# Attention loop on one Trainium2 core: products with the values moved in front of the scores

## What is computed

```python
def proj(W, b):
    return (x @ W.T + b).reshape(Bb, Ss, H, DH).transpose(0, 2, 1, 3)
Q, K, V = (proj(Wq, bq), proj(Wk, bk), proj(Wv, bv))
...
scores = jnp.einsum('bhqd,bhkd->bhqk', Q, K) * scale
...
bias = lam[:, None, None, None] * prior_bias[None, None]
dense_out = jnp.einsum('bhqk,bhkd->bhqd', jax.nn.softmax(scores + bias, axis=-1), V)
...
out = out.transpose(0, 2, 1, 3).reshape(Bb, Ss, Dd)
return out @ Wo.T + bo
```

## Time and profile before

| | |
|---|---|
| median of three runs | 1857.48 us (1856.89 to 1862.09) |
| the profiled execution | 1869.88 us, its span 1868.1 us |
| TensorE | busy 1800.2 us, 96% of the span, mean granted clock 0.979 |
| VectorE | busy 1077.9 us, 58% |
| ScalarE | busy 926.0 us, 50% |
| GpSimd | busy 561.3 us, 30% |
| attention loop | 725.3 to about 1247 us of the span, 256 steps |
| in the window 725 to 1250 us | TensorE busy 514.54 us, VectorE 443.28, ScalarE 446.85 |

### The profile page before, as it was taken

One profiled execution on the slowest core, in us unless ns is written; L12 is line 12 of the kernel. 1 busy time (PEld: TensorE's weight loads), 2 busy tenths in 40 slices (PEclk: granted clock), 3 DMA queues, 4 the chain that ended last, 5 costly groups with the idle time before them and its releaser, 6 DMA issues.

```text
span 1868.1 us, 41317 instructions
## 1 busy us (share of the span) xinstructions
PE 1800.2 (96%) x17131; PEld 1288.8 (69%) x17131; DVE 1077.9 (58%) x2319; ACT 926.0 (50%) x1697; POOL 561.3 (30%) x966
## 2 busy tenths in 40 slices
PE   7989999999999988999999999999999999999997
PEld 3657768565657645777777777766777777777775
DVE  5674644172241256888888788853555544445453
ACT  2313231213343235888888888854555544445512
POOL 3262130042130352121212121103555443455413
PEclk8989999999999989999999999999999999999998
DMA  6100002113353569611113010000000000010001
GB/s 189 26 24 1 4 2 69 72 54 116 102 179 92 162 184 170 95 35 30 33 29 111 21 41 22 22 24 1 2 2 2 2 2 2 2 30 2 2 0 45
DMA packets 89948, 93.55 MB, mean 50 GB/s; under 512 B 35282, under 2 KB 75154, under 8 KB 89618
## 3 DMA queue, kind: packets, MB, share of 16 engines
q1 hardware_dynamic: 83506, 79.12, 15.7%
q0 software_dynamic: 3456, 9.44, 1.9%
q10 hardware_dynamic: 2800, 2.34, 0.4%
HBM read 68.34 MB, written 23.07 MB: 49 GB/s over the span
## 4 chain that ended last, share of the span: by engine, by line
PE 89%; DVE 5%; ACT 2%; DMA 2%; issue 1%; POOL 1%; SPq 0%; POOLq 0%; DVEq 0%; ACTq 0%
PE PS L1870 13%; PE PS L1250 8%; PE PS L1884 7%; PE PS L1259 7%; PE PS L2209 6%; PE PS L1861 6%; PE PS L2287 5%; PE PS L2264 4%; PE PS L2214 3%; PE PS L2248 3%; PE PS L615 2%; PE PS L707 2%; PE PS L2294 2%; PE PS L2326 2%; PE PS L714 2%; PE PS L562 1%
## 5 line engine op out<-in xcount | busy, mean ns | idle before, releaser
L2043 DVE CUSTOM_DVE_ANT_0 arena<-PS,arena 128x1024 f32<-128x1024 f32 x256 | 312.0, 1219 | 63.9 <-PE PS L1861 60.0
L1964 ACT ACTIVATE arena<-arena 128x1024 f32<-128x1024 f32 x256 | 296.7, 1159 | 9.4 <-DVE arena L2043 9.2
L1870 PE MATMUL PS<-arena 128*128 128x128 f32 x2048 | 279.8, 279 | 2.3 <-issue 1.9
L1870 PEld LDWEIGHTS PS<-arena 128*128 128x128 f32 x2048 | 230.5, 142 | 60.2 <-issue 27.0
L2491 POOL TENSOR_SCALAR arena<-arena 128x384 f32<-128x384 f32 (+1 forms) x256 | 143.4, 573 | 251.4 <-DVE arena L2400 251.4
L2372 ACT ACTIVATE arena<-arena 128x385 f32<-128x385 f32 (+1 forms) x256 | 151.4, 593 | 128.6 <-DVE arena L2409 128.6
L1960 ACT COPY arena<-PS 128x512 f32<-128x512 f32 x298 | 170.0, 585 | 63.3 <-PE PS L1870 60.9
L1861 PE MATMUL PS<-arena 96*128 96x512 bf16 x512 | 154.9, 384 | 4.9 <-DVE arena L2043 3.8
L2409 DVE CUSTOM_DVE_ANT_0 arena<-PS,arena 128x384 f32<-128x384 f32 (+1 forms) x256 | 123.2, 538 | 52.3 <-PE PS L2251 39.9
L1250 PE MATMUL PS<-arena 128*128 128x512 f32 x320 | 143.6, 606 | 6.6 <-ACT arena L1395 5.9
L2050 DVE COPY arena<-PS 128x512 f32<-128x512 f32 x214 | 146.9, 687 | 2.3 <-PE PS L1870 2.1
(11 more groups left out here) (340 smaller groups left out, 3079.4 us busy)
## 6 DMA issues: line engine op xcount, KB each, us to landing
arena<-in_L_ffn_W SPq DMA_DIRECT2D x16, 1024.0 KB, 7.5
arena<-prior SPq DMA_DIRECT2D x16, 512.0 KB, 4.2
parts<-arena SPq DMA_DIRECT2D x24, 256.0 KB, 5.1
arena<-parts SPq DMA_DIRECT2D x96, 64.0 KB, 2.9
arena<-parts SPq DMA_DIRECT2D x48, 128.0 KB, 10.6
prior<-arena SPq DMA_DIRECT2D x4, 1024.0 KB, 6.7
ye<-arena SPq DMA_DIRECT2D x7, 512.0 KB, 3.0
ya<-arena SPq DMA_DIRECT2D x7, 512.0 KB, 5.0
```

Source lines behind the costliest of these rows:

```text
L1870: h = e.transpose(PS[:, i, P * j:P * j + P], Sb[z % 3][:, 512 * g + P * j:512 * g + P * j + P], ident)
L1964: e.activation(Sb[z % 3], Sb[z % 3], ACT.Exp, bias=mr[:, z % 4:z % 4 + 1], scale=-1.0).then_inc(s_exp, 1)
L2043: e.tensor_tensor_reduce(Sb[z % 3], ps, Ab[m % 2], 1.0, 3e38, ALU.add, ALU.min, mr[:, z % 4:z % 4 + 1]).then_inc(s_ttr, 1)
```

## The change

In a step with products with the values, TensorE runs them ahead of the scores of that step, and the scores then stand directly ahead of the turn. Before, they stood between the scores and the turn. The instructions are the same, and so is the order on every other engine. In steps without such products (the even ones, and those up to 6), nothing moves.

```diff
         for z in range(NZ + 15):
+            if summed(z):
+                values(*summed(z))
             if z < NZ:
                 scores(z)
-            if summed(z):
-                values(*summed(z))
             if 2 <= z < NZ + 2:
                 turn(z - 2)
             if gathered(z) is not None:
```

## The result

| | before | changed |
|---|---|---|
| median, 20 runs each | 1862.28 us (1856.89 to 1866.73) | 1866.09 us (1862.99 to 1871.78) |
| ratio | 1 | 1.0025, 95% interval 1.0017 to 1.0034 |
| profiled execution's span | 1868.1 us | 1864.1 us |
| V of z = 7 to V of z = 255, in the trace | 492.78 us | 495.32 us |

A forecast was written before the change was run, and what follows sets the result against it. TensorE, busy throughout the attention loop, was taken as the bound. The terms -3.1 + 6.0 + 1.3 + 2.1 gave +6.3 us on the three-run median of 1857.48, so 1863.8, likeliest 1864, range 1855 to 1872.

The forecast's parts named there:

- The case forecast: Attention loop: small crossing gain outweighed by waits, +6.3 us or +0.34%; chance 0.55.
- three places: Waits at the banks of turns' first halves (+6.0 us), two double steps (+1.3), small copy of sums (+2.1).
- the ten steps: Steps z = 23, 39, 71, 87, 119, 143, 147, 183, 215, 231: TensorE idle about 0.6 us each for VectorE's copy.
- crossing, 125 pairs: From products with the values into scores: bare weight load 0.03 instead of 0.06, pair 3.80 to 3.77, -3.1 us.
- bank behind the late copy, 10 pairs: Gather and small closing steps: the even step's turn waits 0.60 us for VectorE's late copy, 6.0 us in all.
- z = 135 and z = 167: Two double steps: closing pieces wait longer on VectorE, +0.5 us at z = 135, +0.75 at z = 167, together +1.3.
- small copy ahead, 14 pairs: ScalarE's small copy of the sums delays its two turn copies by 0.15 us in 14 steps, 2.1 us.
- a load wholly hidden: Faster bound of the crossing term: no weight load lies bare ahead of the scores, -7.1 us.
- its row for the 0.03: First score of the loop: its matmul follows its load by 0.03 us, taken as the bare load.
- The rival of the waiting V: Next products with the values wait for VectorE's copy in 42 pairs, 0.1 us each, 4 us more: 1868; chance 0.15.
- Nothing moves: Same work, two shape crossings per pair, bank waits taken up: time stays at 1857.5 us; chance 0.20.
- The way out is cheap: Values to scores costs no pause or load: 0.15 us saved per pair, 18.8 less 9.4 of waits, 1848; chance 0.10.

The follow-up runs named there:

- e6_only_bank: Changed kernel, ScalarE copying first halves of turns only in gather and closing steps, VectorE in all others; ratio to the kernel before 0.9972, measured again 0.9957.
- e8_before_only: Kernel before with copies dealt out as in e6_only_bank, differing from it only in the place of the scores; ratio to before 0.9996, again 0.9984.
- e1_bank_copies: Changed kernel, ScalarE also copying the turn's first half where a gather or small closing piece takes a bank behind it; ratio to the kernel before 0.9986.
- e7_vector_first: Changed kernel, VectorE copying the turn ahead of the bias step in gather and small closing steps; ratio to the kernel before 1.0009.
- e4_before_both: Kernel before with the edits of e1_bank_copies and e2_sums_later; ratio to the unedited kernel before 1.0007.
- e2_sums_later: Changed kernel, ScalarE's small copy of the sums issued behind the copies of the turn; ratio to the kernel before 1.0009.
- e5_split: e6_only_bank with the products with the values cut in two halves, one ahead of the scores and one behind; ratio to the kernel before 1.0143.
- e9_merged: e6_only_bank with one block of 64 matmuls with the values in every second odd step; ratio to the kernel before 1.011.
- e10_changed_again: The changed kernel measured once more, with no further edit, against the kernel before; ratio 1.0019.

## Why the prediction was right, and where it was off

**The direction and the places.** Forecast was +6.3 us, or 0.34%, slower; measured is 0.25% (0.17 to 0.34%). The case forecast happened: a small gain at the crossing, outweighed by waits in three places, each where it was named. The prediction took 0.3% as the smallest change that can be told from none. The outcome lies just under it, on the side of "same", to which 0.32 was given and to "slower" 0.58; the two could hardly be parted with a forecast so near to the bound. Twenty runs do tell 0.25% from none, so the bound was set too wide. That the time itself, 1866.09, is only 2 us over the forecast 1864 is partly luck: the difference was overestimated by 1.6 us, and the median before moved up from 1857.48 in three runs to 1862.28 in twenty, 4.8 us, so two errors of opposite sign met.

**The signs named for the profile.** Ahead of L1870 in the ten steps, idle time put down to L2050 is there ten times, 0.41 each and not 0.6; the pairs are longer by the 0.60. VectorE's waits for L1861 are 55.6 us in sum, near the 60 named. V does not wait, and no pair is under 3.70.

**Term by term**, in the traces and by the runs:

| term | forecast | in the trace | the run that shows its cause |
|---|---|---|---|
| crossing, 125 pairs | -3.1 us | -5.6 (0.045 a pair) | e6_only_bank against e8_before_only: 4.5 and 5.0 us |
| bank behind the late copy, 10 pairs | +6.0 | +6.0 (4.77 - 4.17 = 0.60 each) | e1_bank_copies, with e7_vector_first and e4_before_both |
| z = 135 and z = 167 | +1.3 | +1.3 (0.53 and 0.70, each + 0.045) | e1_bank_copies |
| small copy ahead, 14 pairs | +2.1 | +2.2 (3.96 - 3.80) | e2_sums_later |
| sum | +6.3 | +3.9 | changed kernel: 4.7 (3.2 to 6.3) |

**The step that was mis-sized** is the way out of V ahead of scores. I took 0.03 of bare weight load in place of 0.06; it is 0.01, so a pair is 3.75 and not 3.77 (the matmuls end 0.61 after the first one's start, against 0.60). The bound that I had written for a load wholly hidden, -7.1 us, was nearer than the -3.1. The rule on weight loads that the prediction names from the Trainium skill, "TensorE: Matmul & The Clock Gate", section LDWEIGHTS (by columns alone), would have put this term at 0, farther off.

The prediction sets its row for the 0.03 aside because "its clock was not the full one". That is misread. From 725.0 to 726.4 us the granted clock is 1.00, and the first score matmul is recorded with 0.38 us as in the loop; only later in those six microseconds does the clock fall. What does set the row apart is that TensorE had stood idle ahead of it, 1.46 us for the load, with no V in front. A row that bears on the term was in the trace before and was not used, the recorded lengths of the weight loads (ns, least/median/longest):

```profile
L1861 PEld LDWEIGHTS PS<-arena x512: 95/99/152, 725.3 to 1232.9; 96*128 96x128 bf16 x171
...
L1870 PEld LDWEIGHTS PS<-arena x2048: 138/141/231, 731.4 to 1238.5; 128*128 128x128 f32 x187
```

Both have 128 columns, and the load of the scores is 0.042 us shorter, about what the bare part shrank by. That one follows from the other is likely but not shown.

**A label that looks like a wait.** The prediction said that V would be seen to wait if the room was gone. In the list of waits of the changed kernel from 850 to 990 us it seems to:

```profile
PEld PS L1884 <- issue: 3.8, 23, 0.2
PEld PS L1861 <- DVE arena L2043: 3.8, 18, 0.2
PEld PS L1861 <- issue: 3.6, 17, 0.2
...
PEld PS L1884 <- DVE arena L2050: 2.0, 12, 0.2
```

Twelve times V's loads are put down to VectorE's copy, L2050. Yet each of these idle times is as long as the 23 put down to "issue", 2.0 / 12 = 3.8 / 23 = 0.17, and the pairs with and without the label have the same length. It is the crossing, at whose end the copy happened to be the last that finished. The rival of the waiting V is thereby out: of the 42 longer pairs that it needs there is none. A real wait of V looks different; there is one at the end of the pair of 4.03 in e1_bank_copies:

```profile
790.48 0.79 PEld L1884 LDWEIGHTS PS<-arena 128*17 128x17 f32 x32 [0.44 <-DVE arena L2050]
```

Here the idle time is 0.44, 0.27 over that of the crossing, and the pair is 0.27 over 3.76. A wait is one only if a distance grows.

**The other rivals.** "Nothing moves" leaned on the number of crossings, which is indeed the same; but their price isn't fixed by the number alone: it depends on what stands on the far side, 0.06 of bare load ahead of a turn and 0.01 ahead of scores. "The way out is cheap" was right in its first half only: the load is free, the pause of about 0.1 stays (e5_split pays it twice), so its 0.15 was never there. What 0.045 a pair is worth once the waits are gone is the distance from e6_only_bank to e8_before_only, 0.24% and 0.27%; the 0.28% and 0.43% by which e6_only_bank beats the kernel before hold about 0.1% from the dealing out of copies as well.

**Left open.** The pairs account for +3.9 us and the ratio gives 4.7; the interval covers both, and the medians lie 3.8 apart. Why the two crossings out of V differ was not isolated. e4_before_both came out a little slow for what its trace shows; its interval holds 1.000, and I did not follow it up.

## What to carry to other kernels

When a piece of work is moved on an engine that is busy all the time, the order of its own instructions is the small part of the account. Ask what the move makes late, and follow that down the hand-written queues of the other engines: here the scores came 1 us later, a copy that had nothing to do with them stood behind them in VectorE's queue, and twelve times in 256 steps TensorE needed that copy or what stood behind it. A regular step with a tenth of a microsecond of room says nothing of the irregular ones; write the step out once for each kind. And when such a change loses a little, look whether the loss sits in a few places: the remedy of one line turned 0.2% slower into 0.3 to 0.4% faster, while on the old order it was worth 0.1%.

## What the runs showed of the hardware that I had not expected

**A crossing between shapes has two prices.** Into 17 columns 0.09 us, as before. Out of them about 0.1 plus the part of the first weight load that lies bare: 0.06 for a float32 turn of 128 columns, at most 0.01 for the bf16 scores, also of 128 columns. The Trainium skill, "TensorE: Matmul & The Clock Gate", section LDWEIGHTS, makes both loads equal; the traces don't agree, neither in the bare part nor in the recorded lengths (0.141 us for float32, 0.099 for bf16). The section "Weight-path perf modes — Fast Weight Load (FWL) and DoubleRow" of the same page of the Trainium skill has a faster load for 128 columns that are not float32, which would fit; no run here separates the type from the rest.

**A stall at one place, of every size.** In the traces of all kernels but e9_merged, which has no V there, the pair from V of z = 27 is longer than its like, whatever the order and the copies. In the trace of e4_before_both, the longest, TensorE stops in the middle of a turn:

```profile
776.07 0.99 PE L1870 MATMUL PS<-arena 128*128 128x128 f32 x7
...
781.96 0.37 PE L1870 MATMUL PS<-arena 128*128 128x128 f32 x1 [4.91 <-issue]
```

The eighth transpose follows 4.91 us of idle time, put down to "issue": TensorE waited for nothing that the profile names. Behind it the granted clock is 0.50 from 782 to 788 us, half of the 1.00 ahead of it, and 1.00 again from 790, so the stall costs more than its own length. This pair and the next are longer than their like by 8.0 us here, by 3.7 in the trace of the kernel before, by 2.2 in the changed one and by 0.2 in e1_bank_copies. It is not a property of a kernel: the changed kernel profiled again (e10_changed_again) lost 1.0, and e6_only_bank 1.4 and then 4.4. So a single execution is moved by more than the effect studied, and only many runs or the pair lengths could show it.

The place is a place in TensorE's instruction stream, not a piece of work. Wherever the idle time shows, it lies ahead of the eighth transpose of T(25), also in e5_split. In e9_merged, where the products come later and in one piece, it lies inside V of z = 29:

```profile
787.09 0.84 PE L1884 MATMUL PS<-arena 128*17 128x128 f32 x20
790.35 2.75 PE L1884 MATMUL PS<-arena 128*17 128x128 f32 x44 [2.42 <-issue]
```

Counted by the program from the loop's first score, the first place lies behind 619 matmuls (56 scores, 352 for the values, 207 of turns, 4 of the gather) and the second behind 618 (58, 340, 216, 4). What TensorE lacks there was not looked for.
